# Last stage of a vision-tower kernel: how the six parts of an expert layer's output row are added up, and who computes the norms' shifts

## The reference, cut to what matters

```
h = h + attn(layernorm(h))          # windows of 64 rows, 8 heads of 16, bias b_proj
# second layernorm and expert layer, E = 8 experts in G = 2 groups, K = 2 chosen
flat = layernorm(layernorm(h)) * ln_scale + ln_bias
out_shared = swiglu(flat @ shared_in_w.T) @ shared_out_w.T + shared_out_b
h_expert   = swiglu(flat @ expert_in_w.T)
routed = cnt @ expert_out_bias
for e in range(E):
    routed = routed + comb[:, e:e+1] * (h_expert @ expert_out_weight[e].T)
return h + out_shared + routed
```

## Time and profile before

| | |
|---|---|
| median of 3 runs | 2762.41 us (2756.27 to 2762.47) |
| profiled execution, its own time | 2761.4 us, of which the trace's span is 2759.4 us |
| busy over the span | DVE 86%, PE 83%, POOL 75%, ACT 59% |
| stage C | from about 1826 us to the end |
| 20 equal turns in stage C (from 1931.2 to 2633.3 us) | 702.1 us, DVE busy 676.65, PE 612.71, POOL 507.30, ACT 366.41 |

### The profile page before, as it was taken

One profiled execution on the slowest core, in us unless ns is written; L12 is line 12 of the kernel. 1 busy time (PEld: TensorE's weight loads), 2 busy tenths in 40 slices (PEclk: granted clock), 3 DMA queues, 4 the chain that ended last, 5 costly groups with the idle time before them and its releaser, 6 DMA issues. The chain is left out here.

```text
span 2759.4 us, 26470 instructions
## 1 busy us (share of the span) xinstructions
PE 2294.0 (83%) x6899; PEld 1098.8 (40%) x6899; DVE 2382.7 (86%) x3555; ACT 1616.4 (59%) x3023; POOL 2068.2 (75%) x1108
## 2 busy tenths in 40 slices
PE   5999999999999999999984148717888888888888
PEld 2444444444444444444432024304444444444444
DVE  3999999999999999999996832226999999999996
ACT  4777777767777777777662124424545555555544
POOL 2889899898898898988992048766777777777772
PEclk8999999999999999999996569857999999999999
DMA  2243333333433333333333013311111111011100
GB/s 75 94 124 99 106 115 105 114 111 93 128 98 108 118 106 110 116 93 115 108 96 98 0 35 73 47 25 31 31 29 30 29 28 31 28 31 31 31 24 23
DMA packets 180609, 199.44 MB, mean 72 GB/s; under 512 B 40062, under 2 KB 170988, under 8 KB 180332
## 3 DMA queue, kind: packets, MB, share of 16 engines
q1 hardware_dynamic: 169196, 189.35, 22.5%
q0 software_dynamic: 11264, 8.40, 2.3%
HBM read 164.44 MB, written 33.25 MB: 72 GB/s over the span
## 5 line engine op out<-in xcount | busy, mean ns | idle before, releaser
L915 POOL TENSOR_TENSOR a_hc<-a_h,a_cs 128x896 f32<-128x896 f32 (+1 forms) x448 | 859.6, 1938 | 55.4 <-DVE a_h L778 54.9
L362 PE MATMUL a_y_bank<-a_hc,a_ident 128*128 128x448 f32 (+1 forms) x1792 | 741.4, 544 | 20.3 <-DVE a_yz L798 19.7
L553 ACT ACTIVATE a_da<-a_dt,a_neg_a 128x448 f32<-128x448 f32 (+1 forms) x896 | 551.8, 631 | 295.6 <-DVE a_h L778 290.6
L778 DVE TENSOR_TENSOR_SCAN a_h<-a_da,a_h,a_dbx 128x448 f32<-128x448 f32 x528 | 583.3, 1135 | 9.5 <-ACT a_da L553 4.4
L362 PEld LDWEIGHTS a_y_bank<-a_hc,a_ident 128*128 128x128 f32 x1792 | 331.6, 190 | 325.2 <-issue 273.0
L2183 POOL TENSOR_TENSOR c_prod<-c_prob,c_qkv 128x1024 f32<-128x1024 f32 x100 | 279.3, 2820 | 189.3 <-DVE c_prob L2053 189.3
L1777 PE MATMUL c_p_E<-c_w_ex,c_hid 128*128 128x512 f32 x800 | 375.4, 599 | 38.3 <-DVE c_sc L2029 36.3
L762 DVE TENSOR_TENSOR a_dbx<-a_dtx,a_b_bank 128x896 f32<-128x896 f32 (+1 forms) x308 | 327.8, 1064 | 15.7 <-PE a_b_bank L355 15.5
L2174 POOL TENSOR_TENSOR c_prod<-c_qkv 128x1024 f32<-128x1024 f32 x100 | 232.7, 2353 | 58.1 <-ACT c_qkv L1845 58.1
L903 POOL TENSOR_TENSOR a_dbp<-a_dtx,a_bs 128x896 f32<-128x896 f32 (+1 forms) x140 | 270.9, 1935 | 0.0
L778 DVE TENSOR_TENSOR_SCAN a_h<-a_da,a_h,a_dbp 128x448 f32<-128x448 f32 x240 | 263.4, 1130 | 0.0
(11 more groups left out here) (306 smaller groups left out, 3744.1 us busy)
## 6 DMA issues: line engine op xcount, KB each, us to landing
a_cs<-c_rows SPq DMA_DIRECT2D x96, 896.0 KB, 5.3
a_bs<-c_rows SPq DMA_DIRECT2D x24, 1120.0 KB, 5.7
a_cs<-c_rows SPq DMA_DIRECT2D x16, 900.0 KB, 4.4
c_x<-h_rows SPq DMA_DIRECT2D x100, 64.0 KB, 2.3
heads<-c_ot SPq DMA_DIRECT2D x25, 256.0 KB, 2.0
c_dealt<-heads SPq DMA_DIRECT2D x200, 32.0 KB, 1.9
rolled<-c_res SPq DMA_DIRECT2D x25, 256.0 KB, 2.4
h_rows<-a_th SPq DMA_DIRECT2D x24, 224.0 KB
```

The costliest lines, as they stand in the source:

```text
L362: pe.matmul(y_bank[:, d, 0:g.w], ident[:], hc[:, (g.i * NS + n) % HC_RING, d, 0:g.w], start=(n == 0), stop=(n == NS - 1)).then_inc(s_sum, 1)
L553: act.activation(da[:, k % DA_RING, 0:g.w], dt[g.slot][:, d, 0:g.w], ACT.Exp, scale=neg_a[:, d * NS + n:d * NS + n + 1]).then_inc(s_da, 1)
L778: dve.tensor_tensor_scan(h[:, n, d, 0:g.w], da[:, (g.i * 2 * NS + k) % DA_RING, 0:g.w], x, state, ALU.mult, ALU.add).then_inc(s_scan, 1)
L915: pool.tensor_tensor(hc[:, (q.i * NS + n) % HC_RING, :, 0:q.w], h[:, n, :, 0:q.w], cs[:, n % C_RING, 0:q.w].unsqueeze(1).to_broadcast([P, ...
```

## The change

The five adds of `total` take the place of the two strided reductions. The bank ACC stays open after `biases`: `total(c, 0)` adds h3 to it in place, `total(c, 1)` to `total(c, 3)` add three of the four expert parts in place, and `total(c, 4)` adds the last one and writes `res`. `keep_acc` is gone, and `parts` has only the experts' four slots in two buffers; h3 has a ring of its own. `by_dve` takes n = 1 and 2 from `by_act`. The shifts are computed by ScalarE, which negates the mean and multiplies by rstd, four ACTIVATEs of one column each. The orders of all engines and of the banks are new, and the store now stands behind `heads_in` in SP's queue.

```diff
             load()
             heads_out()
+            heads_in()
             store_last()
-            heads_in()
@@ scalar @@
             def row_scale2():
                 if N is not None:
                     act.wait_ge(s_mv2, N + 1)
+                    act.activation(minus2[:], mv2[:, :, 0], ACT.Copy, scale=-1.0)
                     act.activation(lnv2[:], mv2[:, :, 1], ACT.Ln, scale=1 + EPS, bias=eps_cols[:, 1:2]).then_inc(s_lnv2, 1)
                     act.wait_ge(s_lnv2, N + 1)
                     act.activation(rstd2[:], lnv2[:], ACT.Exp, scale=-0.5).then_inc(s_rstd2, 1)
+                    act.wait_ge(s_rstd2, N + 1)
+                    for j in range(GT):
+                        i = act.activation(shift2[:, j:j + 1], minus2[:, j:j + 1], ACT.Copy, scale=rstd2[:, j:j + 1])
+                    i.then_inc(s_shift2, 1)
...
-            def keep_acc():
-                    act.copy(parts[X % SUM_RING][:, :, OF_ACC, :], tile_of("acc", X)[:].rearrange("p (j d) -> p j d", j=GT)
-                             ).then_inc(free, 1)
@@ vector @@
         def total(c, k):
-            s = c % SUM_RING
-            taken(dve, "acc", c)
-            dve.wait_ge(s_add, c * GT + 2 * k + 2)
+            acc = tile_of("acc", c)[:].rearrange("p (j d) -> p j d", j=GT)
+            if k == 0:
+                result(dve, "acc", c)
+                dve.tensor_tensor(acc, acc, h3[c % SUM_RING][:], ALU.add).then_inc(s_sum, 1)
+                return
+            dve.wait_ge(s_add, c * GT + GT)
+            dve.wait_ge(s_sum, c * EG + k)
+            part = parts[c % 2][:, :, k - 1, :]
+            if k < EG:
+                dve.tensor_tensor(acc, acc, part, ALU.add).then_inc(s_sum, 1)
+                return
             if c >= 2:
                 dve.wait_ge(s_res[c % 2], (c // 2) * 16)
-            dve.tensor_reduce(res[c % 2][:, 2 * k:2 * k + 2, :],
-                              parts[s][:, 2 * k:2 * k + 2, :, :].rearrange("p j e d -> p j d e"), AX.X, ALU.add
-                              ).then_inc(s_sum, 1)
+            dve.tensor_tensor(res[c % 2][:], acc, part, ALU.add).then_inc(s_free[nth["acc", c][0]], 1)
...
-                    dve.scalar_tensor_tensor(out=shift2[:], in0=mv2[:, :, 0], scalar=-1.0, in1=rstd2[:], op0=ALU.mult,
-                                             op1=ALU.mult).then_inc(s_shift2, 1)
@@ gpsimd @@
             score_products(2)
+            score_products(3)
             add_experts(0)
-            score_products(3)
+            add_experts(1)
             value_products(0)
             value_products(1)
-            add_experts(1)
             add_experts(2)
```

More of the change, by code:

```diff
@@ L1553, in phase_c @@
     marker = sb("marker", [1, 1])
-    lnv, rstd, shift = (sb(n, [P, GT]) for n in ("lnv", "rstd", "shift"))
+    lnv, rstd, minus, shift = (sb(n, [P, GT]) for n in ("lnv", "rstd", "minus", "shift"))
     n3 = sb("n3", [P, GT, D])
@@ L1576, in phase_c @@
     sc = sb("sc", [P, SC_RING, E1, D])
-    parts = [sb(f"parts{s}", [P, GT, SLOTS, D]) for s in range(SUM_RING)]
+    parts = [sb(f"parts{s}", [P, GT, EG, D]) for s in range(2)]
+    h3 = [sb(f"h3{s}", [P, GT, D]) for s in range(SUM_RING)]
     res = [sb(f"res{s}", [P, GT, D]) for s in range(2)]
@@ L1885, in row_scale @@
                     act.activation(rstd[:], lnv[:], ACT.Exp, scale=-0.5).then_inc(s_rstd, 1)
+                    act.wait_ge(s_rstd, L + 1)
+                    for j in range(GT):
+                        i = act.activation(shift[:, j:j + 1], minus[:, j:j + 1], ACT.Copy, scale=rstd[:, j:j + 1])
+                    i.then_inc(s_shift, 1)
             def score_exp():
@@ L1942, in scalar @@
             keep_n3()
-            by_act(0)
             silu(0)
             qkv_copy(0)
+            by_act(0)
             qkv_copy(1)
@@ L1995, in total_last, with total_now @@
                     total(X - 1, k)
+            def total_now(k):
+                if X is not None:
+                    total(X, k)
             def stats_of():
@@ L2007, in stats_of @@
                     i.then_inc(s_mv, 1)
-            def less_mean():
-                if L is not None:
-                    dve.wait_ge(s_rstd, L + 1)
-                    dve.wait_ge(s_mv, L + 1)
-                    need(dve, s_n3, L)
-                    dve.scalar_tensor_tensor(out=shift[:], in0=mv[:, :, 0], scalar=-1.0, in1=rstd[:], op0=ALU.mult,
-                                             op1=ALU.mult).then_inc(s_shift, 1)
             def hidden(i):
@@ L2138, in vector @@
             choose_experts()
-            total_last(0)
+            by_dve(1)
+            hidden(0)
             sum_values(N, 2)
-            hidden(0)
+            total_last(1)
             sum_values(N, 3)
+            total_last(2)
             sum_scores(0)
-            total_last(1)
-            sum_scores(1)
             stats_of()
             hidden(1)
+            total_last(3)
+            sum_scores(1)
+            total_last(4)
             sum_scores(2)
             choose_group()
+            by_dve(2)
+            hidden(2)
             sum_scores(3)
@@ L2152, in vector @@
             add_rows()
+            probs()
             by_dve(4)
-            probs()
-            hidden(2)
-            less_mean2()
             by_dve(5)
-            less_mean()
             hidden(3)
             by_dve(6)
+            sum_values(A, 0)
             by_dve(7)
-            sum_values(A, 0)
+            total_now(0)
             sum_values(A, 1)
-        for k in range(2):
+        for k in range(1, EG + 1):
             total(NG - 1, k)
```

72 lines of the change are left out of this document (32 added, 40 removed), and 8 rows, old and new, of the table BANK_ORDER.

## The result

The median fell from 2762.22 to 2675.23 us, a ratio of 0.969 [0.9674, 0.9707]: 87 us less, against 84 forecast (2678, range 2660 to 2714). The profiled execution has a span of 2672.2 us.

What follows compares the result with a forecast made beforehand. VectorE's list bounded the 35.1 us turn; shortened to 29.3 it leaves TensorE's 30.8, plus 0.4 for waits: 31.2. Twenty turns save 78 us, the next two 4.7, so 2761.4 - 83 = 2678 us, range 2660 to 2714.

Steps and rivals of the forecast that it cites:

- What sets the turn: In stage C, TensorE's list without its waits, 30.8 us, would bound the turn, so the gain is at most 4.3 us.
- 0.4 for waits: Added to each turn for waits that don't overlap as engines hand work to each other, making 31.2 us.
- VectorE's list: VectorE's work per turn falls from 35.1 to 29.3 us (above: 31.0), with adds and evictions at 0.6 us.
- The shifts: VectorE's two 128x4 shifts wait for GpSimd's products through two SBUF inputs; removing them takes 4.5 us off its list.
- The sums: On VectorE, two strided sums of 5.5 us a turn give way to five adds of 3.0 us (above: 4.7).
- The heads' way: From turn_o to the projection's end 10.2 to 10.7 us, heads_in 0.5 to 0.9 sooner; no gain counted, no slack.
- ScalarE: Its total doesn't grow; ten small ACTIVATEs of 0.21 to 0.29 us; second norm hidden with some 1 us to spare.
- GpSimd: 28.0 us a turn, below TensorE; 5.1 us from the fourth score product to the next probabilities, half filled by two adds.
- The tail: The last turn has four adds for one strided sum and a late shared: 1 us lost at most.
- The lock: Rival: VectorE's less_top subtraction and probs' multiply held by GpSimd's adds, up to 1.28 us each; 2706 us; chance 0.2.
- TensorE never waited for the bank ACC: Rival: ACC held until total(c, 4) delays shared and the projection; turns 33 to 34.5 us, time 2730; chance 0.07.
- The adds didn't wait as the shifts had: Rival: VectorE's five adds wait for GpSimd; at 1.5 us each the time is 2795 us, slower; chance 0.03.

Runs made afterwards that it cites:

- e5: The changed kernel with the eviction by_dve(4) ahead of probs on VectorE, as it stood before; 2681.66 us, turn 31.3.
- e7: The changed kernel with GpSimd's order as before, one add between the third and fourth score product; 2692.94 us, turn 32.0.
- e2: The kernel before, shifts still on VectorE but in two instructions, the negated mean going to PSUM first; 2713.47 us, turn 32.95.
- e1: The kernel before with only the two shifts moved to ScalarE; 2716.71 against 2759.29 us, turn 32.95.
- e3: The changed kernel with both shifts back on VectorE, one behind the probabilities, one behind the second eviction after them; 2679.96 us, turn 31.0.
- e8: The changed kernel with the two strided sums and ScalarE's bank copy back in place of the five adds; 2724.12 us, turn 33.45.
- e4: The changed kernel with the store ahead of heads_in in SP's queue, as before; 2726.5 us, turn 33.4.
- e6: e1 with the changed kernel's GpSimd order, both adds of experts behind the fourth score product; 2710.2 us, turn 32.8.
- e10: The changed kernel with sum_values(N, 3) and the statistics ahead of the first part add, total(c, 0) ahead of by_dve(6); 2661.65 us.
- e11: The changed kernel with e10's moves, first score sum behind the first part add, second value product's sum ahead of the next turn's first eviction; 2657.97 us.

## Why the prediction was right, and which step was not

- **The time.** 31.2 us a turn was forecast, 30.88 measured; 2678 against 2675. The right total comes in part from a wrong step, next.
- **What sets the turn: wrong.** "Without them its own list takes 35.1 - 4.3 = 30.8 us", and "at most 35.1 - 30.8 = 4.3" with 0.4 for waits. TensorE's list proved to be 29.8, a mis-sized term: the prediction took the list of the old order for the new one, in which the same up-projections alone take 0.58 us a turn less. TensorE was busy 96% with waits of 1.1 us a turn, where 98% and under 1 us were to be seen if its list set the turn. The 4.2 us gained are 35.1 less 30.88, the mean of turns that mostly take the 30.7 of the rings of GpSimd and VectorE. e5 and e7 show it: a longer ring with unchanged lists makes the turn longer by that amount. That 30.8 and 30.7 are so near is chance. The sum knew engines' lists only and put the rest into "0.4 us a turn for waits that don't overlap".
- **VectorE's list: right.** 29.3 forecast and found; adds at 0.69 us, from start to start 0.6 (2164.28 to 2164.89), and evictions at 0.687.
- **The shifts: mechanism right, worth misread.** The 2.3 us are a wait that needs two SBUF inputs (e2). But a saving in the list is not one in the turn: taken alone it gives 35.1 - 32.95 = 2.1 of its 4.5 us (e1), and on top of the rest 0.25 to 0.3 (e3). I had expected e3 to lose most of its gain. By turns: before 35.1, shifts alone 32.95, all but the sums 33.45, all but the shifts 31.0, all 30.7. The parts don't add up, since the turn stops each time at whatever is longest next.
- **The sums: larger than their list.** 2.7 us a turn with everything else in place (e8), for 2.5 in the list.
- **The heads' way: right and decisive.** It takes 10.45 us from the start of `turn_o` (2166.28) to the end of the projection (2176.73), with 10.2 to 10.7 forecast. "No slack either": e4 costs 2.5 us a turn, where the prediction gave the exchange of the two issues 0.5 to 0.9 us on the way and counted nothing for it.
- **ScalarE: right.** A shift column takes 0.283 us, within 0.21 to 0.29, four of them 0.85 together. The rows of the second norm are ready some 0.6 us before TensorE asks (about 1 us forecast).
- **GpSimd.** 25.4 of work, and one short wait between the two adds at the end (0.92 us in this turn); the wait for the probabilities fell from 7.9 to 4.5 us. 28.0 as a list was no bound, but its order is half of the ring (e7: 1.3 us). It came out short as well: from the end of the fourth score product (2173.48) to the end of the probabilities it took 7.8 us, not 5.1, since VectorE was busy with other steps and came to the last score sum only at 2176.05. That is where the sum of lists missed that VectorE was behind GpSimd.
- **The tail.** 1 us was allowed, 3.5 were lost, with a granted clock of 0.93 in the last stretch (0.96 before). The cause is open.
- **Rivals.** The lock did not move to the subtraction: 0.425 us in the changed kernel, since both of GpSimd's adds were over (2176.88) before the subtraction (2177.75); e6 shows 1.03 where they meet. TensorE never waited for the bank ACC. The adds didn't wait as the shifts had: one of their two inputs is in PSUM.

## What to carry to other kernels

When in-order engines hand work to each other several times a turn, compare the turn not only with each engine's list but with each ring: from a wait on engine A to what released it on B, along B without a pause back to B's last wait, and so on until the same step of the turn before. Here 0.6 and 1.3 us put into the ring cost the turn as much, with no list changed (e5, e7). Taking work out gains only up to the next ring or list: nothing with two of three rings left (e10), 0.4 us with all of them opened (e11). Work that stands outside the ring was nearly free (e3: both shifts for 0.25 us). A tiny VectorE instruction that takes microseconds is worth a look at where its inputs lie and what GpSimd runs then: one input in PSUM did as well here as another engine (e2, e1), and a place just before GpSimd starts nearly as well (e3).

## What the runs showed of the hardware

- The same VectorE instruction of 128x4 with both inputs in SBUF took 0.156 us ahead of GpSimd's product, and 0.71 and 2.3 us beside one (e3 and before). Beside one it ended with the product: the earlier trace rows, and in e3 at 2152.41, where the first of two products begun at 2149.57 (5.63 us together) ended near 2152.4.
- VectorE can add in place in an open PSUM bank at the price of an eviction (0.69 us for 128x512), also beside GpSimd's products (2155.61, beside the two products of 2150.59 to 2156.23). The strided reduction costs 2.83 / 1536 = 1.84 ns an element against 1.212 / 1024 = 1.18 for the reduction of `sum_values`.
- ScalarE's one-column ACTIVATEs take 0.283 us each, but four in a row 0.85 us, 0.19 from start to start.
